# Layer 1 of a four-layer network: TensorE makes the attention scores of batch 0 between the first products of the two batches

## The chip, the cores and the metric

The kernel runs on one NeuronCore of a Trainium2 chip. The metric is the device time of one execution in microseconds (us). The kernel before takes 1194.64 us, the median of three runs (1191.98 to 1196.13).

## The reference

x is (2 batches, 1024 tokens, 256 features), float32. Four layers follow each other, each of the form x = x + ffn(cond(x)). Layer 0 conditions by a low-rank adapter and a layernorm, layers 2 and 3 by a linear map picked by an id of the batch; the ffn parts are mixtures of experts (8 experts in layers 0 to 2, 32 and a shared one in layer 3). The change lies in the conditioning of layer 1, an attention pooling:

```python
attn_in = tanh(einsum('bsd,da->bsa', hidden, W1) + b1)      # a = 64
scores  = einsum('bsa,a->bs', attn_in, v)
mask    = prefix, postfix or all-but-self, by an id of the batch  # (b, 1024, 1024)
p       = softmax(where(mask, scores[:, None, :], -1e30))
pooled  = einsum('bjl,bld->bjd', p, hidden) / count(mask)
```

Layer 1's ffn then routes each pooled token to the one expert with the largest logit (pooled @ Wr + br), with exact gelu, and scales by the gate.

## The kernel before

All of x stays in SBUF as 16 tiles of 128 tokens (x_tok). Work goes by four chunks of 512 tokens: chunks 0 and 1 are batch 0, chunks 2 and 3 batch 1. A product that has to be as exact as float32 is made as three of a cheaper type: each operand is split into a high and a low part, and hi x hi, hi x lo and lo x hi are added (helper mm3, lines 810 to 812; the low parts come from VectorE, line 1653).

Each engine runs its own list of instructions in the order that is written out, and waits on semaphores. There is no planner. For layer 1's conditioning the lists are:

- TensorE: two small products for layer 2's router (L1219, L1222), 32 transposes of x (L822), then for each chunk the attention rows: 6 products, K = 128 features in two halves, 72 output rows (64 of the attention's first matrix and 8 of the router's) by 512 tokens. Chunk c goes to PSUM bank 4 + c. Then for each chunk the scores: 4 matmuls against the vector v give them as columns (L1240, two records each), and one against v broadcast to 128 columns gives the same scores as a row on all 128 partitions (L1242, two records). After chunks 1 and 3 the semaphore s_sc is raised. Then 16 small transposes of the router's rows (L1246) and, batch by batch, the products of the pooling (L1268 to L1280, and mm3).
- ScalarE: the high parts of the transposed x (L1358), then for all four chunks tanh (L1579) and a copy of the 8 router rows (L1580) out of the bank into hidden_f, raising s_chf once for each chunk. Only behind these four pairs stand, for each batch, the copies of the score columns (L1584) and of the score row (L1585), which wait for s_sc. After that the exponentials of the pooling.
- VectorE: the low parts of the transposed x, v broadcast over 128 columns (L2519, raises s_clo), then the splits of x for the pooling (L2530), then the prefix and suffix maxima of batch 0's score row as two scans (L2550, L2551), row maxima, the router's columns (L2539, need the 16 transposes), arguments of the exponentials (L2584), carry_out (L2593, waits for the score rows of both batches), and the same again for batch 1.
- SyncE stores the pooled rows (z_rows) chunk by chunk, and GpSimd gathers them by expert once the slots are known (L701).

The lines that matter for ScalarE's order (1577 to 1585):

```python
for c in range(NC):
    act.wait_ge(s_ch, CH0[1] + c + 1)
    act.activation(HF[0:A0, c, :], PS[0:A0, 4 + c, :], ACT.Tanh, bias=CB1[:, 0:1])
    act.activation(HF[A0:A1R, c, :], PS[A0:A1R, 4 + c, :], ACT.Copy).then_inc(s_chf, 1)
for b in range(B):
    act.wait_ge(s_sc, b + 1)
    bs = slice(b * TPB, (b + 1) * TPB)
    act.activation(SM[:, 0, bs], PS[:, 4 + b, bs], ACT.Copy)
    act.activation(SC[:, 2 * b:2 * b + 2, :], PS[:, 2 * b:2 * b + 2, :], ACT.Copy).then_inc(s_sc_sb, 1)
```

Of the kernel before, what the change touches and what calls it, by code (L numbers as in the profile page):

```python
# [27 lines left out]
NC = B * SEQ // CH  # L28
TPC = CH // P
KD = D // P  # L30
# [37 lines left out]
def build(nc, t):  # L68

    with ExitStack() as ctx:  # L70
# [3 lines left out]
        def sem(name):  # L74
            return ctx.enter_context(nc.semaphore(name))
# [214 lines left out]
        TR0 = {n: KD * NC * i for i, n in enumerate(TR)}  # L290
# [4 lines left out]
        s_tlo = sem("tr_lo")  # L295
# [4 lines left out]
        s_clo = sem("cond_lo")  # L300
        CHI0 = {0: 0, 3: NC}
        CLO0 = {0: 0, 1: NC, 3: NC + 1}
# [504 lines left out]
        def _(pe):  # L807
            def mm3(out, lh, ll, rh, rl, first, last):

                nc.tensor.matmul(out, lh, rh, start=first, stop=False)  # L810
                nc.tensor.matmul(out, lh, rl, start=False, stop=False)  # L811
                return nc.tensor.matmul(out, ll, rh, start=False, stop=last)  # L812
# [410 lines left out]
            last.then_inc(s_red, 1)  # L1223
            transposes("x1", X, lambda c: pe.wait_ge(s_x[c], 16 * 2))
            pe.wait_ge(s_csplit, 2)
            for c in range(NC):
                pe.wait_ge(s_tlo, TR0["x1"] + KD * (c + 1))
                for k in range(KD):
                    w = slice(k * A1R, (k + 1) * A1R)
                    last = mm3(PS[0:A1R, 4 + c, :], W1h[:, 1, w], W1l[:, 1, w], TAh[:, k, c * CH:(c + 1) * CH],  # L1230
                               TAl[:, k, c * CH:(c + 1) * CH], k == 0, k == KD - 1)
                last.then_inc(s_ch, 1)

            pe.wait_ge(s_tlo, TR0["x1"] + KD * NC)
            pe.wait_ge(s_clo, CLO0[1] + 1)
            for c in range(NC):

                pe.wait_ge(s_chf, c + 1)
                for j in range(TPC):
                    nc.tensor.matmul(PS[:, 4 + c // 2, c * TPC + j:c * TPC + j + 1], HF[0:A0, c, j * P:(j + 1) * P],  # L1240
                                     V1[:], start=True, stop=True)
                last = nc.tensor.matmul(PS[:, c, :], SC[0:A0, 7, 0:P], HF[0:A0, c, :], start=True, stop=True)  # L1242
                if c % 2:
                    last.then_inc(s_sc, 1)
            for n in range(NT):
                last = nc.tensor.transpose(PS[:, 6, n * 8:(n + 1) * 8], HF[A0:A1R, n // TPC, n % TPC * P:(n % TPC + 1) * P],  # L1246
                                           ident[A0:A1R, A0:A1R])
# [1481 lines left out]
```

## Time and profile before

| what | value |
|---|---|
| median of 3 runs | 1194.64 us (1191.98 to 1196.13) |
| the profiled execution, time | 1195.43 us |
| its span in the profile | 1193.8 us |
| TensorE matmul busy | 1041.9 us, 87% |
| VectorE busy | 924.3 us, 77% |
| ScalarE busy | 651.1 us, 55% |
| GpSimd busy | 559.4 us, 47% |
| mean granted TensorE clock | 0.921 |

The busy shares say which engine works most over the whole span, the chain of waits which work ended last at each moment, and the timelines what stood idle for what. The granted clock is the share of TensorE's full speed that the chip allowed: 1.00 is 2.4 GHz, 0.50 is 1.2 GHz. Layer 1's attention scores lie near 641 us of the span. In the timelines, a row that ends in brackets gives the idle time before it and what ended that.

### The profile page before, as it was taken

The numbers are of one execution on the slowest core, as the hardware profiler recorded it, in microseconds if no ns is written. First come the engines' busy times: TensorE is split into PE (matmuls) and PEld (weight loads), VectorE is DVE, ScalarE is ACT, GpSimd is POOL, SyncE is SP. The second block draws the span as 40 slices with busy tenths as digits, with TensorE's granted clock in tenths as the row PEclk, the third lists the DMA queues.
The fourth block names the chain that finished last, engine by engine and source line by source line (L and its number), as shares of the span: only waits on it lengthen the run. The fifth ranks groups of instructions, "written<-read, shape, count | busy, mean of one in ns | idle before, by whom it ended". The sixth has DMA issues, their size and how long they took to land.

```text
span 1193.8 us, 26110 instructions
## 1 busy us (share of the span) xinstructions
PE 1041.9 (87%) x7813; PEld 986.1 (83%) x7813; DVE 924.3 (77%) x1570; ACT 651.1 (55%) x1407; POOL 559.4 (47%) x375
## 2 busy tenths in 40 slices
PE   7249999999999999999978749999769958888896
PEld 5238999999999999999966649999669955777785
DVE  7877888888888888888847768875758864967695
ACT  4227776767676767676724447763357625224221
POOL 1312878887888788888740033443046720000000
PEclk9568999999999999999986859999879979999898
DMA  7346787877787777777632167562368743030202
GB/s 216 108 166 207 219 243 215 247 231 234 223 242 234 228 230 235 241 222 234 189 44 71 48 219 266 202 221 84 105 203 261 238 154 122 14 89 24 94 14 71
DMA packets 85093, 206.22 MB, mean 173 GB/s; under 512 B 16738, under 2 KB 58482, under 8 KB 71218
## 3 DMA queue, kind: packets, MB, share of 16 engines
q1 hardware_dynamic: 60530, 161.45, 40.2%
q0 software_dynamic: 24512, 44.19, 15.2%
q8 instruction: 20, 0.33, 0.1%
q14 instruction: 31, 0.25, 0.1%
HBM read 170.85 MB, written 34.75 MB: 172 GB/s over the span
## 4 chain that ended last, share of the span: by engine, by line
PE 73%; DVE 10%; issue 6%; DMA 6%; ACT 2%; POOL 2%; DVEq 0%; POOLq 0%; SPq 0%; ACTq 0%
PE ps L810 22%; PE ps L811 22%; PE ps L812 22%; PE ps L905 2%; DMA z_tok<-in_L_w 1%; DMA w_raw<-z_rows,slot_rows 1%; PE ps L822 1%; DMA y_rows<-w_raw,slot_rows 1%; PE ps L867 1%; DVE hidden_lo L1653 1%; DVE x_tok L1985 1%; POOL w_raw L701 1%; DVE featB_lo L1653 1%; DMA z_tok<-y_rows 1%; DMA x_rows<-w_raw,slot_rows 1%
## 5 line engine op out<-in xcount | busy, mean ns | idle before, releaser
L1419 ACT ACTIVATE hidden_f<-ps,b_block 128x256 f32<-128x256 f32 x480 | 247.6, 516 | 195.0 <-PE ps L812 193.0
L701 POOL DMA_INDIRECT x_tok<-z_gate_rows,slot_rows x88 | 240.4, 2732 | 127.4 <-DVE block_gates L1943 70.2
L1420 ACT ACTIVATE hidden_hi<-ps,b_block 128x256 fp32r<-128x256 f32 x480 | 249.7, 520 | 0.0
L810 PE MATMUL ps<-w_hi,featA_hi 128*128 128x256 f32 (+2 forms) x724 | 209.0, 289 | 8.8 <-DVE scratch L2334 5.5
L811 PE MATMUL ps<-w_lo,featA_hi 128*128 128x256 f32 (+2 forms) x724 | 207.9, 287 | 0.0
L812 PE MATMUL ps<-w_hi,featA_lo 128*128 128x256 f32 (+2 forms) x724 | 207.9, 287 | 0.0
L810 PE MATMUL ps<-featB_hi,hidden_hi 128*128 128x256 f32 x712 | 203.3, 286 | 3.3 <-DVE hidden_lo L1653 3.3
L811 PE MATMUL ps<-featB_lo,hidden_hi 128*128 128x256 f32 x712 | 201.1, 282 | 0.0
L812 PE MATMUL ps<-featB_hi,hidden_lo 128*128 128x256 f32 x712 | 199.7, 280 | 0.0
L1653 DVE TENSOR_TENSOR hidden_lo<-hidden_f,hidden_hi 128x512 fp32r<-128x512 f32 x276 | 178.0, 692 | 17.3 <-ACT hidden_hi L1420 15.6
L729 POOL DMA_INDIRECT x_rows<-w_raw,slot_rows x88 | 145.8, 1657 | 39.9 <-issue 29.0
L810 PEld LDWEIGHTS ps<-w_hi,featA_hi 128*128 128x128 f32 (+2 forms) x724 | 141.1, 195 | 10.6 <-issue 6.3
L811 PEld LDWEIGHTS ps<-w_lo,featA_hi 128*128 128x128 f32 (+2 forms) x724 | 141.3, 195 | 0.4
L812 PEld LDWEIGHTS ps<-w_hi,featA_lo 128*128 128x128 f32 (+2 forms) x724 | 141.3, 195 | 0.3
L810 PEld LDWEIGHTS ps<-featB_hi,hidden_hi 128*128 128x128 f32 x712 | 134.4, 189 | 3.7 <-DVE hidden_lo L1653 3.7
L812 PEld LDWEIGHTS ps<-featB_hi,hidden_lo 128*128 128x128 f32 x712 | 134.6, 189 | 0.0
L811 PEld LDWEIGHTS ps<-featB_lo,hidden_hi 128*128 128x128 f32 x712 | 134.0, 188 | 0.0
L701 POOL DMA_INDIRECT w_raw<-z_rows,slot_rows x44 | 54.3, 1233 | 158.0 <-DVE slot_rows L1818 76.8
L1927 DVE TENSOR_TENSOR w_raw<-ps,b_block 128x256 f32<-128x256 f32 x132 | 54.7, 418 | 69.2 <-PE ps L812 66.7
L1653 DVE TENSOR_TENSOR featA_lo<-scratch,featA_hi 128x2048 fp32r<-128x2048 f32 (+3 forms) x50 | 91.4, 1829 | 3.2 <-ACT featA_hi L1541 2.4
L810 PE MATMUL ps<-w_hi,featB_hi 128*128 128x256 f32 x288 | 84.9, 295 | 8.9 <-DVE w_lo L1653 6.3
L719 POOL DMA_INDIRECT y_rows<-w_raw,slot_rows x44 | 56.5, 1284 | 60.8 <-DVE w_raw L1927 48.4
(487 smaller groups left out, 2591.6 us busy)
## 6 DMA issues: line engine op xcount, KB each, us to landing
scratch<-in_L_w SPq DMA_DIRECT2D x54, 1024.0 KB
z_tok<-in_L_w SPq DMA_DIRECT2D x32, 1024.0 KB
x_tok<-in_L_w SPq DMA_DIRECT2D x22, 1024.0 KB
b_block<-in_L_ffn_b POOLq DMA_DIRECT2D x66, 128.0 KB
z_tok<-y_rows SPq DMA_DIRECT2D x12, 512.0 KB, 5.6
z_tok<-in_L_w SPq DMA_DIRECT2D x12, 512.0 KB
scratch<-in_L_w SPq DMA_DIRECT2D x12, 512.0 KB
z_rows<-z_tok SPq DMA_DIRECT2D x8, 512.0 KB, 2.9
```

What stands on the lines that cost most here:

```text
L701: gp.indirect_dma_start(XBL[L][:, k, tt, :], None, ZD if L else ZD0, bass.IndirectOffsetOnAxis(ap=TOK[:, q * BTT + tt:q * BTT + tt + 1], a ...
L719: gp.indirect_dma_start(YD, bass.IndirectOffsetOnAxis(ap=TOK[:, q * BTT + tt:q * BTT + tt + 1], axis=0), YB[:, k, tt, :], None).then_inc(s ...
L729: gp.indirect_dma_start(XD, bass.IndirectOffsetOnAxis(ap=TOK[:, q * BTT + tt:q * BTT + tt + 1], axis=0), YB[:, k, tt, :], None, compute_op ...
L810: nc.tensor.matmul(out, lh, rh, start=first, stop=False)
L811: nc.tensor.matmul(out, lh, rl, start=False, stop=False)
L812: return nc.tensor.matmul(out, ll, rh, start=False, stop=last)
L822: last = nc.tensor.transpose(PS[:, g % 4, j * P:(j + 1) * P], src[:, c * TPC + j, k * P:(k + 1) * P], ident[:])
L905: last = nc.tensor.transpose(PS[:, 6 + k, m * BT + tt * P:m * BT + (tt + 1) * P], XBL[L][:, k, tt, m * P:(m + 1) * P], ident[:])
L1419: act.activation(HF[:, f // 2, part], ps, func, bias=b1)
L1420: act.activation(HTh[:, k, f // 2, part], ps, func, bias=b1).then_inc(s_hhi[L], 1)
L1653: return nc.vector.tensor_tensor(out, full, hi.bitcast(F32), ALU.subtract)
L1927: nc.vector.tensor_tensor(YB[:, k, j, :], PS[:, 4 + j, 0:D], B2B[:, k, :], ALU.add).then_inc(s_yev[L], 1)
```

## The change

The loops over four chunks on TensorE become two functions. The rows of chunks 0 and 1 are made first, then the two waits for x's low parts and for v, then the scores of chunks 0 and 1, then rows of chunks 2 and 3, then their scores. The instructions are the same, and no other engine's list changes.

```diff
--- before.py
+++ after.py
@@ -1223,7 +1223,7 @@
             last.then_inc(s_red, 1)
             transposes("x1", X, lambda c: pe.wait_ge(s_x[c], 16 * 2))
             pe.wait_ge(s_csplit, 2)
-            for c in range(NC):
+            def attention_rows(c):
                 pe.wait_ge(s_tlo, TR0["x1"] + KD * (c + 1))
                 for k in range(KD):
                     w = slice(k * A1R, (k + 1) * A1R)
@@ -1231,10 +1231,7 @@
                                TAl[:, k, c * CH:(c + 1) * CH], k == 0, k == KD - 1)
                 last.then_inc(s_ch, 1)
 
-            pe.wait_ge(s_tlo, TR0["x1"] + KD * NC)
-            pe.wait_ge(s_clo, CLO0[1] + 1)
-            for c in range(NC):
-
+            def scores(c):
                 pe.wait_ge(s_chf, c + 1)
                 for j in range(TPC):
                     nc.tensor.matmul(PS[:, 4 + c // 2, c * TPC + j:c * TPC + j + 1], HF[0:A0, c, j * P:(j + 1) * P],
@@ -1242,6 +1239,17 @@
                 last = nc.tensor.matmul(PS[:, c, :], SC[0:A0, 7, 0:P], HF[0:A0, c, :], start=True, stop=True)
                 if c % 2:
                     last.then_inc(s_sc, 1)
+
+            attention_rows(0)
+            attention_rows(1)
+            pe.wait_ge(s_tlo, TR0["x1"] + KD * NC)
+            pe.wait_ge(s_clo, CLO0[1] + 1)
+            scores(0)
+            scores(1)
+            attention_rows(2)
+            attention_rows(3)
+            scores(2)
+            scores(3)
             for n in range(NT):
                 last = nc.tensor.transpose(PS[:, 6, n * 8:(n + 1) * 8], HF[A0:A1R, n // TPC, n % TPC * P:(n % TPC + 1) * P],
                                            ident[A0:A1R, A0:A1R])
```

## Rows read from the trace of the kernel before

**Rows 1.** The page, part 4: shares by engine of the chain that ended last.

```profile
PE 73%; DVE 10%; issue 6%; DMA 6%; ACT 2%; POOL 2%; DVEq 0%; POOLq 0%; SPq 0%; ACTq 0%
```

**Rows 2.** Chain of waits, 625 to 700 us: start us, us, what.

```profile
644.22 1.57 PE ps L1242 x2
645.81 0.18 ACT small L1584
645.99 0.92 ACT scratch L1585
646.93 2.29 DVE z_tok L2550
649.23 2.19 DVE z_tok L2551
...
687.79 2.90 DMA z_rows<-z_tok
```

**Rows 3.** Timeline of GpSimd, 680 to 705: start, us, instruction, idle before and releaser.

```profile
700.60 1.03 POOL L701 DMA_INDIRECT w_raw<-z_rows,slot_rows  x1 [76.80 <-DVE slot_rows L1818]
```

**Rows 4.** Timeline of TensorE around the change, 618 to 665.

```profile
630.13 5.75 PE L822 MATMUL ps<-ident,x_tok 128*128 128x128 f32 x32 [2.69 <-DMA x_tok<-x_rows]
635.64 0.47 PE L810 MATMUL ps<-featA_hi,w_hi 128*72 128x512 f32 x1
...
638.29 0.39 PE L812 MATMUL ps<-featA_hi,w_lo 128*72 128x512 f32 x1
...
641.09 0.39 PE L812 MATMUL ps<-featA_hi,w_lo 128*72 128x512 f32 x1
641.41 1.05 PE L1240 MATMUL ps<-cond_v,hidden_f 64*128 64x1 f32 x8
...
643.27 0.95 PE L1240 MATMUL ps<-cond_v,hidden_f 64*128 64x1 f32 x8
644.08 1.69 PE L1242 MATMUL ps<-hidden_f,scratch 64*128 64x512 f32 x2
645.57 1.70 PE L1240 MATMUL ps<-cond_v,hidden_f 64*128 64x1 f32 x8
...
648.98 1.70 PE L1240 MATMUL ps<-cond_v,hidden_f 64*128 64x1 f32 x8
```

**Rows 5.** Timeline of ScalarE, 632 to 665.

```profile
637.92 0.68 ACT L1579 ACTIVATE hidden_f<-ps,cond_b 64x512 f32<-64x512 f32 x1
638.62 0.59 ACT L1580 ACTIVATE hidden_f<-ps 8x512 f32<-8x512 f32 x1
...
642.55 0.59 ACT L1580 ACTIVATE hidden_f<-ps 8x512 f32<-8x512 f32 x1
645.81 0.18 ACT L1584 ACTIVATE small<-ps 128x8 f32<-128x8 f32 x1 [2.67 <-PE ps L1242]
...
652.71 1.02 ACT L1585 ACTIVATE scratch<-ps 128x1024 f32<-128x1024 f32 x1
```

**Rows 6.** Timeline of VectorE, 618 to 665.

```profile
627.56 0.21 DVE L2519 COPY scratch<-cond_v 64x128 f32<-64x128 f32 x1
...
634.48 3.18 DVE L1653 TENSOR_TENSOR featA_lo<-ps,featA_hi 128x512 fp32r<-128x512 f32 x5 [0.17 <-ACT featA_hi L1358]
...
644.20 1.23 DVE L1653 TENSOR_TENSOR w_lo<-x_tok,w_hi 128x1024 fp32r<-128x1024 f32 x1
646.93 2.29 DVE L2550 TENSOR_TENSOR_SCAN z_tok<-scratch 128x1024 f32<-128x1024 f32 x1 [1.51 <-ACT scratch L1585]
...
655.75 0.26 DVE L2539 CAST featB_hi<-ps 128x96 fp32r<-128x96 f32 x1
...
657.79 1.27 DVE L2593 SCALAR_TENSOR_TENSOR hidden_f<-scratch,carry_col,carry_out_mask 16x1024 f32<-16x1024 f32 x1
```

**Rows 7.** Stretches around the change: from:to, us, busy us, PEclk, DMA share, GB/s.

```profile
630.10:634.20 4.10, 4.07 (x19) 4.07 (x20) 1.96 (x3) 2.15 (x4) 0.00 (x0) 0.50 1.00 321
641.10:644.40 3.30, 3.30 (x21) 2.45 (x20) 3.23 (x5) 1.99 (x4) 0.00 (x0) 1.00 0.00 0
644.50:652.60 8.10, 8.10 (x23) 4.81 (x22) 6.45 (x9) 1.09 (x2) 0.00 (x0) 0.50 0.00 0
```

**Rows 8.** Timeline of TensorE in layer 3's conditioning, 975 to 986.

```profile
985.25 0.63 PE L810 MATMUL ps<-featB_hi,w_hi 128*128 128x512 f32 x1
985.68 0.45 PE L811 MATMUL ps<-featB_lo,w_hi 128*128 128x512 f32 x1
```

**Rows 9.** Stretches of dense products at the lower clock in layers 1 and 2.

```profile
723.00:726.30 3.30, 3.30 (x18) 3.30 (x17) 3.27 (x3) 3.18 (x9) 0.00 (x0) 0.50 0.92 367
```

## The prediction

> **What bounds the kernel now.** I read the page's part on the chain that ended last first [rows 1]: TensorE carries 73% of it, so the kernel as a whole is a TensorE kernel. That share says little about the place of the change. So the second view is the chain of waits between layer 0's last scatter and layer 1's first gather [rows 2]. There the reader sees the chain walk from TensorE's score products (L1240, L1242, until 645.8 us) to ScalarE's copy of them out of PSUM (L1584, L1585), then to VectorE's two scans (L2550, L2551) and, 40 us of pooling later, to the store of the last pooled rows (687.79). Nothing in layer 1's experts can begin earlier: GpSimd's first gather waited 76.8 us for the slots that come out of it [rows 3]. A shift of the first scan is thus a shift of the end.
>
> The third view is the timeline of the three engines around the change [rows 4 to 6]. TensorE runs 24 products of the attention rows without a gap (635.64 to 641.09, one each 0.233 us), then the scores of chunks 0, 1, 2, 3. ScalarE, in its own order, loads a table (until 637.92), does tanh and copy of chunks 0 to 3 (pairs 1.31 us apart, the last over at 643.14), and then sits until 645.81. VectorE splits x until 645.43 and idles 1.51 us for the copied score row. So three things end late here, in this order: VectorE's splits 645.43, TensorE's second score 645.77, and the copy.
>
> **The change part by part.** No instruction is added or taken away: 12 row products (chunks 2, 3) move behind the scores of chunks 0 and 1, and two waits move forward with the scores. No DMA is issued by TensorE, so no queue of SP or GpSimd is passed. ScalarE's order is untouched, and that decides the case: its copy of batch 0's scores stands behind tanh and copy of chunks 2 and 3, which now wait for products that TensorE makes last.
>
> Step 1, TensorE reaches the first score. Chunk 1's last row product starts at 638.29 and ends near 638.7 [rows 4]. The score of chunk 0 needs ScalarE's pair for chunk 0, over at 638.62 + 0.59 = 639.21 [rows 5]. TensorE idles about 0.6 us; the table load in front of tanh sets it, not TensorE. The other two waits are free: the last of x's transposed low parts is over at 634.48 + 3.18 = 637.66, and the broadcast vector was made at 627.56 [rows 6]. First score at 639.3 instead of 641.4.
>
> Step 2, the scores of chunks 0 and 1. At full clock one chunk costs 643.27 - 641.41 = 1.86 us, at the lower clock 648.98 - 645.57 = 3.41 us [rows 4]. At full clock they are over at 639.3 + 2 x 1.86 = 643.0, and chunk 1's input (640.52) is there in time. That is 2.8 us earlier than 645.77, and nobody can use it, since ScalarE is not yet at its copy.
>
> Step 3, the rows of chunks 2 and 3: 12 products, 0.233 us each at full clock, 0.43 us at the lower one, from the same shape in layer 3's conditioning [rows 8]. Which level holds is the main unknown. What the rows show: the granted clock stood at 1.00 (2.4 GHz) up to 644.4 and at 0.50 (1.2 GHz) from 644.5 [rows 7], though TensorE never idled half a microsecond in that time. It fell 3.1 us after the last wide product had ended (near 641.3), during scores whose first operand has 64 rows and, in L1240, one column. Back at full level it came at 634.2, 4.1 us after 32 dense transposes had begun [rows 4, 7]. The change puts the same thin scores right behind 12 wide products, with 0.6 us of idleness ahead of them. Two ends:
> - Early fall, the same 3.1 us after the last wide product of chunk 1: 641.6. Then 24% of chunk 1's score at full clock and 76% x 3.41 = 2.6 us at the lower: over at 644.2. The 12 products from 644.2: until a rise 4.1 us later (648.3) there are 9.5 of them, the other 2.5 take 0.6 us: 648.9, and 0.2 us until the last result stands.
> - Late fall, where it was, 644.4: the scores end at 643.0, chunk 2's six products at 644.4, chunk 3's take 6 x 0.43 = 2.6: 647.0, and 0.2.
>
> Step 4, ScalarE. Chunk 2's pair is hidden behind chunk 3's products in both. After the last row product come tanh and copy of chunk 3, 1.3 us, then the score copy. It starts at 649.1 + 1.3 = 650.4 (early fall) or 647.2 + 1.3 = 648.5 (late), instead of 645.8: +4.6 or +2.7 us. VectorE had been waiting for just this copy, so its splits hide none of it. I take the middle, +3.7, since nothing in the rows puts the fall nearer to one end.
>
> Step 5, what follows. Batch 1's scores start near 648.2, behind the row products, and end at 652 at full clock or near 655 at the lower (2 x 3.41 us); their copy is over 1.2 us later, by 656.2. In before it ended at 653.73 [rows 5], and VectorE first needs it at 657.79 [rows 6], in carry_out, a point that moves back by the same 3.7 us to 661.5: 5 us of room, cost 0; if that cover were gone, each microsecond of it would show. The 16 small transposes behind them are needed at 655.75 [rows 6], which moves back too. The pooling is a chain of VectorE and ScalarE, with TensorE's sums of batch 1 released by it; that the clock level meets them at another place I cost at 0, between -1 and +1.
>
> Sum: -0.6 x 0 (TensorE's idleness is off the chain), -2.8 earlier scores x 0, +3.7 later copy = +3.7 us. Profiled execution: 1195.43 + 3.7 = 1199.1. That execution lies 0.79 above the median of 1194.64; against the median 1198.3.
>
> A rule that speaks against this. By the rows, the clock fell at 644.4 with TensorE at work all the time [rows 7]. The Trainium skill (TensorE: Matmul & The Clock Gate, section on why this matters for your kernels) says that long idle gaps between bursts of matmuls are what loses the full clock. By that rule the 0.6 us of waiting would cost nothing and the second batch's rows would run at full clock (the first rival); the trace of before disagrees with it in this very stretch. The same page, section on the back-to-back issue gap, gives some 131 ns for each 512-column matmul; by it the 12 products would take 1.6 us, ScalarE's own two pairs would be the bound (644.0 + 2 x 1.3 = 646.6) and the delay only 0.8 us; the rows show 0.233 us each.
>
> **The rivals.**
> - A, the clock stays full through chunks 2 and 3. For: 12 wide products arrive soon after the scores. Against: it fell in before in a like stretch. The products end at 643.0 + 12 x 0.233 + 0.2 = 646.0, the copy starts at 647.3: +1.5, 1196.1.
> - B, the delay does not reach the end: some later wait has slack. For: layer 1's weights also land after the pooling. Against: their loads are issued behind it, and the gather waited for it [rows 3]. +0, 1194.6.
> - C, faster than before: layer 1's and 2's experts begin at another point of the clock's levels. Dense work of TensorE ran at the lower level at 709.4 to 712.7, 723.0 to 726.3 and 842.5 to 845.8 [rows 9]; each such stretch costs half of 3.3 = 1.65 us. If all three vanish, 3 x 1.65 = 4.95 against +3.7: -1.25, so 1193.4. It decides from the third on. Against: as many new ones can appear.
> - D, batch 1 suffers too: scores and small transposes run at the lower clock and late enough that carry_out waits, 2 us more: +5.7, 1200.3. Against: the room of step 5.
> That the change fails to do what it says is not likely: TensorE has one order, and it is written out.
>
> **How the numbers follow.** Chances: forecast 0.68, A 0.13, B 0.07, C 0.05, D 0.07. What can be told from no change is about 0.3%, 3.6 us. The forecast's own range, 1196.9 to 1199.7, lies on both sides of 1198.2: a little over half of it (0.37) and D count as slower, the other 0.31, A and B as same, which gives 0.44 and 0.51; C and scatter give faster 0.05. The range for 8 in 10 takes in A, most of D and the spread of 4 us among the three times of before: 1194.3 to 1200.9.
>
> **What would show it.** Right: the first L1240 near 639.3; ScalarE's tanh of chunk 2 waiting for TensorE (L812); batch 0's copy (L1585) between 648.5 and 650.5; the first scan equally later; the last store of z_rows later by the same amount; the clock at 0.50 in part of the stretch of chunks 2 and 3. Wrong: the first scan before 646.9 (then ScalarE's order is not what holds it), or a first scan 3 us later with a store of z_rows at its old time (slack that I missed), or the clock at 1.00 until 646 (A).

## The result and the profile after

The changed kernel takes 1199.87 us (median of 8 runs, 1196.76 to 1201.93) against 1194.64 us (8 runs). The ratio to the kernel before is 1.0035, 95% interval 1.002 to 1.005: slower by 4.2 us (2.4 to 6.0); the two medians themselves lie 5.2 us apart. The forecast was +3.7, or 1198.3 us against the median, with a range of 1194.3 to 1200.9.

The two profiled executions differ by only 2.4 us of span, because they were not alike ahead of the change: after began its first transpose of x 1.62 us earlier. So everything below is counted from that transpose (630.13 before [rows 4], 628.51 after). The change has no part in that difference: four variants of the kernel before and of the changed one (e4, e6, e11, e1), whose lists are unchanged up to there, began it at 626.5 to 626.8. The chain of waits of after, start us, us, what:

```profile
641.38 1.92 PE ps L1239 x2
...
648.44 0.59 ACT hidden_f L1588
649.05 0.18 ACT small L1592
649.23 0.92 ACT scratch L1593
650.18 2.29 DVE z_tok L2558
```

Where before the chain went from the score straight to ScalarE's copy [rows 2], tanh and copy of chunk 3 (L1587, L1588) now stand between. (Lines moved: L1237 and L1239 are the old L1240 and L1242, L1587 to L1593 the old L1579 to L1585, L2558 the first scan, the old L2550.) The timeline of TensorE after:

```profile
628.51 5.80 PE L822 MATMUL ps<-ident,x_tok 128*128 128x128 f32 x32 [2.69 <-DMA x_tok<-x_rows]
...
636.71 0.39 PE L812 MATMUL ps<-featA_hi,w_lo 128*72 128x512 f32 x1
637.85 1.02 PE L1237 MATMUL ps<-cond_v,hidden_f 64*128 64x1 f32 x8 [0.75 <-ACT hidden_f L1588]
638.74 1.15 PE L1239 MATMUL ps<-hidden_f,scratch 64*128 64x512 f32 x2
639.68 1.70 PE L1237 MATMUL ps<-cond_v,hidden_f 64*128 64x1 f32 x8
641.25 2.05 PE L1239 MATMUL ps<-hidden_f,scratch 64*128 64x512 f32 x2
643.23 0.70 PE L810 MATMUL ps<-featA_hi,w_hi 128*72 128x512 f32 x1
...
645.86 0.63 PE L810 MATMUL ps<-featA_hi,w_hi 128*72 128x512 f32 x1
...
647.31 0.40 PE L812 MATMUL ps<-featA_hi,w_lo 128*72 128x512 f32 x1
```

The timelines of ScalarE and of VectorE after:

```profile
638.42 0.59 ACT L1588 ACTIVATE hidden_f<-ps 8x512 f32<-8x512 f32 x1
646.10 0.68 ACT L1587 ACTIVATE hidden_f<-ps,cond_b 64x512 f32<-64x512 f32 x1 [7.09 <-PE ps L812]
...
649.05 0.18 ACT L1592 ACTIVATE small<-ps 128x8 f32<-128x8 f32 x1
```

```profile
642.69 1.23 DVE L1661 TENSOR_TENSOR w_lo<-x_tok,w_hi 128x1024 fp32r<-128x1024 f32 x1
650.18 2.29 DVE L2558 TENSOR_TENSOR_SCAN z_tok<-scratch 128x1024 f32<-128x1024 f32 x1 [6.26 <-ACT scratch L1593]
```

And the clock in three stretches after (from:to, us, busy us by engine, PEclk, DMA share, GB/s):

```profile
632.80:639.60 6.80, 6.05 (x36) 4.29 (x35) 6.55 (x13) 5.92 (x10) 0.00 (x0) 1.00 0.01 2
639.70:646.40 6.70, 6.70 (x19) 3.87 (x18) 4.15 (x5) 0.30 (x1) 0.00 (x0) 0.50 0.00 0
646.50:653.20 6.70, 5.99 (x41) 3.96 (x40) 3.02 (x2) 4.32 (x8) 0.00 (x0) 1.00 0.00 0
```

The reader is to see four things. TensorE's scores of batch 0 are over about when the next row product starts, 643.23, and ScalarE doesn't touch them for nearly 6 us: it sits 7.09 us in front of chunk 2's tanh, and its copy comes at 649.05. The level (the granted clock, 1.00 or 0.50) fell near 639.7, as chunk 1's score began, where before it fell within that score's second part, L1242 [rows 4, 7], and 7.5 of the 12 late row products ran at 0.43 us each. VectorE's wait for the score row grew from 1.51 us [rows 6] to 6.26. And the scan stands 21.67 us after the first transpose instead of 16.80: +4.87.

Followed on in the same count: the copy of the last pooled rows starts at 60.94 instead of 56.07, +4.87; GpSimd's first gather at 75.76 instead of 70.47 [rows 3], +5.29. From the gather to the end the profiled execution took 491.9 us against 493.2. So -1.6 ahead of the change, +5.3 to the gather, -1.3 behind it make the +2.4 of the two spans. Only the middle term can be tied to the change. The last one is no larger than what two executions of one kernel differ by: in e5, the changed kernel again, the stretch from the gather to the end took 495.2 us.

### The profile page after: what moved, and what is told of

Same layout as the page of the kernel before. It is cut to its first block, busy times and chain, and to the rows that moved or that the text cites. A ratio compares the mean times of both kernels' runs of the same rounds, so it can differ in the third digit from the quotient of the medians.

```text
span 1196.2 us, 26110 instructions
## 1 busy us (share of the span) xinstructions
PE 1035.9 (87%) x7813; PEld 981.3 (82%) x7813; DVE 924.4 (77%) x1570; ACT 649.7 (54%) x1407; POOL 556.7 (47%) x375
## 4 chain that ended last, share of the span: by engine, by line
PE 70%; DVE 11%; DMA 7%; issue 6%; ACT 3%; POOL 1%; POOLq 1%; DVEq 0%; SPq 0%; ACTq 0%
PE ps L810 22%; PE ps L811 21%; PE ps L812 21%; DMA y_rows<-w_raw,slot_rows 2%; PE ps L905 2%; DMA z_tok<-in_L_w 1%; PE ps L822 1%; DVE featA_lo L1661 1%; PE ps L867 1%; POOL w_raw L701 1%; DVE hidden_lo L1661 1%; DMA z_tok<-y_rows 1%; DMA x_rows<-w_raw,slot_rows 1%; DVE x_tok L1993 1%; DMA w_raw<-z_rows,slot_rows 1%
```

## The experiments

Each was timed in 5 rounds beside the kernel before. The table counts from the first transpose of x in each profiled execution, in us; the ratio is of the times.

Two cautions for the table. The kernel before was profiled once. In e11 nothing differs from it until behind the first scan, and there the scan stands at 17.23 and not at 16.80: the level fell 13.8 us after the first transpose instead of 14.3, ahead of chunk 1's score row (L1242) and not within it. So a difference of 0.4 us between two profiles says nothing by itself. The level must also be alike on both sides of a comparison: in the changed TensorE order it fell 11.2 us after the first transpose in two profiles (changed, e10) and stayed at 1.00 until 20.5 us or later in four (e5, e1, e8, e9), leaving out e3 and e7 with fillers among the scores.

| kernel | first scan | last pooled rows' copy | ratio to before, 95% interval |
|---|---|---|---|
| before | 16.80 | 56.07 | |
| changed | 21.67 | 60.94 | 1.0035 (1.002 to 1.005) |
| e5 changed, again | 18.27 | 57.53 | 1.0039 (1.0016 to 1.0062) |
| e1 ScalarE's order too | 15.10 | 56.07 | 0.9983 (0.9968 to 0.9998) |
| e10 the same, again | 15.94 | 55.61 | 0.9984 (0.9965 to 1.0002) |
| e8 copies behind chunk 2 | 16.82 | 56.13 | 1.0003 (0.9987 to 1.0019) |
| e2 three chunks first | 18.86 | 58.19 | 1.001 (0.9993 to 1.0027) |
| e3 filled | 19.13 | 58.63 | 1.003 (1.0009 to 1.005) |
| e7 both orders, filled | 15.10 | 56.01 | 1.0001 (0.9986 to 1.0017) |
| e6 ScalarE's order alone | 17.24 | 58.39 | 1.0014 (0.9997 to 1.003) |
| e4 copy later | 20.80 | 60.12 | 1.0018 (1.0003 to 1.0034) |
| e9 both orders, pooling filled | 15.06 | 55.37 | 0.9988 (0.9974 to 1.0003) |
| e11 pooling filled alone | 17.23 | 56.49 | 1.0008 (0.9993 to 1.0024) |

**e1, ScalarE's order changed to match.** 

> The changed TensorE order, and ScalarE's list changed to match: tanh and copy of chunks 0 and 1, the copies of batch 0's scores, tanh and copy of chunks 2 and 3, the copies of batch 1's scores. My theory (the loss is ScalarE's copy of batch 0's scores standing behind tanh of chunks 2 and 3, whose products TensorE now makes last): the copy starts when the scores of chunk 1 are over, and the first scan starts when VectorE's splits of x end. Counted from the first transpose of x, the scan was at 16.8 us before and at 21.7 after; here at 15.3 to 15.5. Time 1.4 us under before, 1193.2, some 5.5 under the changed kernel. Rival (TensorE's own order and clock make the loss, whatever ScalarE does): the scan stays near 21 us and the time near 1199.

```diff
-            for c in range(NC): (tanh and copy of chunk c)
-            for b in range(B): (copies of batch b's scores)
+            attention_tanh(0); attention_tanh(1); score_row(0)
+            attention_tanh(2); attention_tanh(3); score_row(1)
```

ScalarE's timeline:

```profile
636.28 0.59 ACT L1588 ACTIVATE hidden_f<-ps 8x512 f32<-8x512 f32 x1
639.48 0.18 ACT L1593 ACTIVATE small<-ps 128x8 f32<-128x8 f32 x1 [2.61 <-PE ps L1239]
```

The first transpose is at 626.59 here: the score copy starts at 12.9 and the scan at 15.10, 0.2 earlier than expected, with VectorE idle no more. The whole of the changed kernel's delay is gone, with TensorE's new order left in. But the level stayed at 1.00 here, and in the changed kernel's first profile it fell, so this pair alone doesn't say how much of the 6.6 us is ScalarE's order. Two pairs with the level alike do: e5 and e1, both at 1.00, have the scan at 18.27 and 15.10 (3.2 us), and the changed kernel and e10, both with the fall at 11.2, at 21.67 and 15.94 (5.7 us; rows at e10). The theory stands and the rival falls. The time is 2 us under before where 1.4 were expected, but the last pooled rows came no earlier than before; e9 looks into that.

**e8, the copies one place later.** 

> The changed TensorE order, ScalarE's copies of batch 0's scores behind tanh and copy of chunk 2 and ahead of those of chunk 3. My theory: the copy waits for six of the late row products and one pair: it starts between 15.6 (full clock) and 18 us (lower clock) after the first transpose, against 15.75 before and 20.6 in the changed kernel; first scan 16.7 to 19, time between -0.1 and +2.3, 1195.8 on average. Rival (position in ScalarE's list is all or nothing): either as the first experiment (15.1) or as the changed kernel (21.7).

```diff
-            score_row(0)
-            attention_tanh(2)
+            attention_tanh(2)
+            score_row(0)
```

The scan at 16.82, between the two, and the time is that of before. The copy starts at 15.7 us, against 15.6 expected for the full level, which this profile has. With the level at 1.00 in all three, the scan stands at 15.10 with the copies behind no late chunk (e1), at 16.82 behind one and at 18.27 behind both (e5): each place in ScalarE's list behind a late chunk costs; it is not all or nothing.

**e2, three chunks first.** 

> TensorE makes the rows of chunks 0, 1 and 2, then the scores of chunks 0 and 1, then the rows of chunk 3, then the other scores. ScalarE's order as in before. My theory: the copy waits for six late products instead of twelve. Rows of three chunks end 4.2 us after the first product, the scores of chunks 0 and 1 at 8.3 to 9.3, the rows of chunk 3 at 9.9 (full clock) to 11.9 (lower clock), then 1.3 us of tanh and copy of chunk 3: the score copy 0.9 to 3.0 us later than before, about half of the changed kernel's delay; time +2, 1196.6. Rival (any split of the row products costs the same, since the wait in front of the first score or the clock's fall is what is paid): +4.

```diff
             attention_rows(1)
+            attention_rows(2)
 ...
-            attention_rows(2)
             attention_rows(3)
```

The scan at 18.86, +2.06 with six late products instead of twelve, all six at the lower level. That is within the expected 0.9 to 3.0. But in e5 (18.27) none and in the changed kernel's first profile (21.67) 7.5 of the late products were slow, so no profile at this one's level tells whether the delay is halved. Time +0.1% (1.2 us), interval from -0.8 to +3.2: it agrees, but the time alone would not tell it from no change.

**e3, fillers to keep the clock up.** 

> The changed kernel with five wide products more (128 x 72 x 512, results never read): three in TensorE's wait ahead of the first score, two between the scores of chunks 0 and 1. If about half of the delay is the lower clock during the rows of chunks 2 and 3, as the prediction has it, and wide products keep the clock up, the twelve row products run at 0.233 us each; the two fillers behind the first score cost 0.5 us themselves: first scan 1.5 + 0.5 = 2 us later than before instead of 4.9, time 1196.6, 3 us under the changed kernel. Rival (the clock has no part in it, or fillers don't hold it): the time is that of the changed kernel or 0.5 us over it.

```diff
             pe.wait_ge(s_clo, CLO0[1] + 1)
+            (3 wide products)
             scores(0)
+            (2 wide products)
             scores(1)
```

The stretch from the rise to the end of all scores, and the scan (first transpose at 627.65):

```profile
631.50:648.40 16.90, 16.90 (x92) 10.52 (x90) 12.66 (x19) 10.29 (x18) 0.00 (x0) 1.00 0.01 1
```

```profile
646.78 2.29 DVE L2562 TENSOR_TENSOR_SCAN z_tok<-scratch 128x1024 f32<-128x1024 f32 x1 [3.94 <-ACT scratch L1597]
```

The level stayed at 1.00 and the scan came at 19.13, +2.3 where 2 were expected. But e5 (next) shows that the changed kernel can keep the level without fillers, so this one profile doesn't prove that the fillers held it, and the time (+0.3%) is not told apart from the changed kernel's. The mechanism's size is shown by e5, the cure is not.

**e5, the changed kernel again.** 

> The changed kernel once more, beside the variants of this call and on their chip. My theory: ratio to the kernel before near 1.0035, +4.2 us; first scan 3.0 to 4.9 us later than before, counted from the first transpose of x (16.8 before), by where the clock falls. Rival (its loss was scatter of the first measurement): ratio at or under 1.001.

No edit. The clock around the change, and the scan (first transpose at 628.24):

```profile
632.10:649.00 16.90, 16.18 (x96) 10.65 (x94) 13.52 (x20) 11.08 (x18) 0.00 (x0) 1.00 0.00 1
649.20:659.20 10.00, 2.65 (x13) 1.76 (x14) 9.51 (x27) 2.19 (x5) 0.00 (x0) 0.50 0.00 0
```

```profile
646.51 2.29 DVE L2558 TENSOR_TENSOR_SCAN z_tok<-scratch 128x1024 f32<-128x1024 f32 x1 [3.08 <-ACT scratch L1593]
```

The same kernel, with the level full through all twelve late products: +1.47 at the scan and +1.46 at the last pooled rows. That is the prediction's rival A to a tenth (+1.5), below what was expected here (3.0 to 4.9), while the ratio repeats, 1.0039. The level is thus a matter of the execution, not of the kernel: 3.4 us lie between the two profiles of one kernel. (Against e11's 17.23 instead of before's 16.80 the delay here would be 1.0 us.)

**e6, ScalarE's order alone.** 

> TensorE's order as in the kernel before, ScalarE's list as in the first experiment: batch 0's score copies ahead of tanh and copy of chunks 2 and 3. My theory (each order must match the other): the copy waits for TensorE's score of chunk 1 as in before, first scan at 16.8 us; chunk 3's tanh is some 6 us later, which delays batch 1's scores to about 27 us, still ahead of their use at 27.7: +0 to +1. Rival (ScalarE's order alone brings what the first experiment gained): -1.4 or more, 0.9988.

The edit of e1 on the kernel before. VectorE's timeline (first transpose at 626.84):

```profile
644.08 2.29 DVE L2558 TENSOR_TENSOR_SCAN z_tok<-scratch 128x1024 f32<-128x1024 f32 x1 [2.06 <-ACT scratch L1586]
...
654.37 0.26 DVE L2547 CAST featB_hi<-ps 128x96 fp32r<-128x96 f32 x1 [1.50 <-PE ps L1246]
```

No gain: the scan at 17.24, and a new wait of 1.50 us for the 16 small transposes behind batch 1's late scores. Those I had thought still in time. The 0.4 at the scan is the lower clock in chunk 1's score, as in e11, and not the edit's. The 2.3 us at the last pooled rows are over the expected 1, the time +0.14% is within reach of it. The rival falls: neither order brings anything alone.

**e4, the copy made later without touching TensorE.** 

> The kernel before, with nothing changed on TensorE; ScalarE copies batch 0's score row four more times, to places nobody reads, ahead of the copy that VectorE waits for: 4 x 0.93 = 3.7 us. My theory (a shift of the first scan is a shift of the end): first scan +3.7, time +3.7, 1198.3. Rival (the delay of the scan is taken up by slack later, and the changed kernel's loss comes from TensorE's clock levels further on): less than +1.5.

```diff
+                if b == 0:
+                    (4 copies of PS[:, 0:2, :] to unused places)
                 act.activation(SC[:, 2 * b:2 * b + 2, :], PS[:, 2 * b:2 * b + 2, :], ACT.Copy).then_inc(s_sc_sb, 1)
```

The scan +4.00, the last pooled rows +4.05: no slack up to there. (Against e11, which has the same fall of the level in chunk 1's score, +3.57 and +3.63; the four copies took 3.6.) The time moved by +0.18%, 2.2 us, interval 0.4 to 4.1, which holds the expected 3.7 but also much less. Up to the pooled rows the passing on is shown; that all of it reaches the end is made likely, not shown, by the times.

**e7, both orders and the fillers.** 

> Both orders changed as in the first experiment, and the five wide products of the third. My theory: the score copy is gated by the scores of chunk 1, half a microsecond later for the two fillers (13.5 instead of 13.0 us), still under VectorE's splits of x, so the first scan stays at 15.1 to 15.3; the clock at full level has nothing left to give on the path: the same time as the first experiment, 0.998 to 0.999. Rival (the clock level kept up helps the pooling behind it): another 1 us or more under it.

The edits of e1 and e3 together. Scan 15.10 as expected, last pooled rows 56.01, time 1.0001 instead of 0.998 to 0.999. The rival, a further gain, falls. A loss of some 2 us against e1 is not told apart from scatter (the intervals overlap).

**e9, the clock kept up in the pooling.** 

> The first experiment's kernel (both orders changed), and in each batch's pooling five products more of 128 x 16 x 240, results never read, behind the first half's twelve wide products, where TensorE idled 0.95 us for the carry. In the first experiment's trace the scan was 1.7 us earlier than before, and the copy of the last pooled rows at the same 56.07 us after the first transpose: the clock fell to 0.50 at 678.0, in the middle of the last 24 products, whose ends VectorE waited 4.41 us for instead of 2.74. Theory (the first experiment's gain is given back there): with the clock kept up the last pooled rows come at 54.4 to 54.6, time 1.6 under the first experiment, 1192 to 1192.5. Rival (the fall there is not prevented or the five products delay the carry): 56 to 56.5, time as the first experiment or a little over.

```diff
+                    if h == 0:
+                        (5 products 128 x 16 x 240 to unused columns)
                     pe.wait_ge(s_plow, plow("carry", b))
```

In e1 the last 24 products straddled a fall:

```profile
671.30:677.90 6.60, 5.64 (x44) 5.00 (x43) 3.88 (x11) 2.85 (x6) 0.00 (x0) 1.00 0.00 0
678.10:682.00 3.90, 3.89 (x17) 3.33 (x15) 0.00 (x0) 1.11 (x4) 0.00 (x0) 0.50 0.39 134
```

and VectorE waited 4.41 us for them, 1.6 longer than in the other profiles, except for e7, the same order with its fillers, where the level fell at the same place and the wait was 4.37:

```profile
677.01 0.16 DVE L2620 TENSOR_TENSOR small<-ps,small 128x4 f32<-128x4 f32 x1 [1.83 <-PE ps L1288]
682.02 0.16 DVE L2620 TENSOR_TENSOR small<-ps,small 128x4 f32<-128x4 f32 x1 [4.41 <-PE ps L1288]
```

With the five products (e9) the level stayed full there, but the rise before it came 3.2 us later in the count, so the first half was the late one:

```profile
678.05 0.16 DVE L2624 TENSOR_TENSOR small<-ps,small 128x4 f32<-128x4 f32 x1 [2.73 <-PE ps L1292]
681.38 0.16 DVE L2624 TENSOR_TENSOR small<-ps,small 128x4 f32<-128x4 f32 x1 [2.74 <-PE ps L1292]
```

The last pooled rows at 55.37: 0.7 of the 1.7 us arrive, not 1.5. Neither theory has it whole. Nor is it shown that the five products kept the level: e10, without them, has it full there as well and a wait of 2.73. The two kernels' times, 0.9988 and 0.9984 (e10), are alike.

**e10 and e11, the controls of e9.** 

> The first experiment's kernel once more, to be compared in one call with the one that fills the pooling, and because one measurement gave 0.9983 and the variant with five wide products in front gave 1.0001. Theory (the scan's 1.7 us are mostly given back in batch 1's pooling): ratio 0.998 to 1.000, last pooled rows at 56 us after the first transpose. Rival (the whole 1.7 us arrive): 0.9986 or less with the last pooled rows at 54.5.

e10 is e1's kernel once more. Its level fell as chunk 1's score began, so the scan came at 15.94 and the last pooled rows at 55.61:

```profile
637.84 1.02 PE L1237 MATMUL ps<-cond_v,hidden_f 64*128 64x1 f32 x8 [0.75 <-ACT hidden_f L1588]
639.68 1.70 PE L1237 MATMUL ps<-cond_v,hidden_f 64*128 64x1 f32 x8
643.22 0.70 PE L810 MATMUL ps<-featA_hi,w_hi 128*72 128x512 f32 x1
```

```profile
643.33 0.18 ACT L1593 ACTIVATE small<-ps 128x8 f32<-128x8 f32 x1 [4.32 <-PE ps L1239]
```

The first transpose is at 628.51, as in the changed kernel's first profile, and TensorE's rows are those of that profile to 0.02 us, through the fall, the rise and the last late product. Only ScalarE's order differs, and its copy starts at 643.33 instead of 649.05. That is the comparison that shows the cause: 5.7 us, with TensorE's order and clock alike. The ratio repeats, 0.9984, which theory and rival both allowed; the last pooled rows lie nearer to the theory's 56, with 0.5 of 0.9 us arriving. What makes the 2 us in the times of e1 and e10 is therefore not shown by their profiles, where the last pooled rows gained 0 and 0.5.

> The kernel before with the five products in each pooling alone. Theory: in the trace of before the clock was full through batch 1's last products, so there is nothing to gain: ratio 1.000, last pooled rows at 56.1 us after the first transpose, within 0.2. Rival (the pooling's clock matters in most executions of before as well): 1.5 us under it.

The fillers on the kernel before bring nothing: 1.0008. The last pooled rows came at 56.49, outside the expected 0.2 about 56.1, because the scan itself was 0.43 later here.

## Why the prediction was right

Steps counted from the first transpose, predicted (early-fall case) and measured in the changed kernel's first profile:

| step | predicted | measured |
|---|---|---|
| TensorE idle ahead of the first score | 0.6 | 0.75 |
| first score | 9.2 | 9.34 |
| clock falls | 11.5 | 11.2 |
| late row products start | 14.1 | 14.72 |
| clock rises again | 18.2 | 18.0 |
| batch 0's copy starts | 20.3 | 20.54 |
| delay of the scan | +4.6 (late fall +2.7, rival A +1.5) | +4.87; in e5 +1.47 |
| delay of the last pooled rows | as the scan | +4.87; in e5 +1.46 |
| time | +3.7 | +4.2 (2.4 to 6.0) |

- **ScalarE's place (steps 2 and 4)** was the cause. e1 and e10 take the loss away by ScalarE's list alone, e10 with TensorE's timeline the same as in the changed kernel's first profile; e8 takes away about half of what e1 does at the same level. TensorE's earlier scores were worth nothing as predicted, since nobody could take them.
- **The level during the late rows (step 3)** was costed as one number between two ends. It is two cases of one kernel, +4.87 and +1.47, and neither profile shows a delay near the middle, +3.7; that this figure came near the measured +4.2 is in part luck. The forecast and rival A were not rivals but two executions of the same program. I gave A 0.13, and of the six profiles whose TensorE list is the changed one up to the late rows four had the level full through the late rows. How often each comes is open: the ratios 1.0035 and 1.0039 would suggest instead that the costly one is the more common. In the two that fell, the level had also risen later, 4.3 us after the first transpose against 3.8 or less; why, the runs don't say.
- **The sizes within step 3** offset each other. The late products began 0.6 us later than costed, and the rise came 3.3 us behind their start instead of 4.1, so 7.5 of them were slow and not 9.5. The 3.1 us from the last wide product to the fall, taken over from before, were 2.7 in the first profile; in e5 the level stood on through chunk 1's score and the late rows.
- **The rule against it.** The Trainium skill (TensorE: Matmul & The Clock Gate, section on why this matters for your kernels) gives long idle gaps between bursts of matmuls as what loses the full clock. The changed kernel's first profile does not agree: the level fell at 639.7 with an idle gap of 0.75 us in front. Nor can its contrary be said outright, since in e5 the same order kept it, with a gap of 0.59. The late row products ran 0.233 us apart in e5, as costed for the full level.
- **The passing on (step 5)**: +4.87 became +4.87 at the last pooled rows and the first gather was 5.29 later; e4 shows the same up to the pooled rows. Batch 1's scores were in time, as costed, but the room is smaller than I made it where they come late: in e6 the 16 transposes behind them were 1.50 us late, which I had named as covered. How much of the delay reaches the end of the kernel is told by the times alone, and only within their intervals.
- **The pooling at another clock phase, costed at 0 between -1 and +1**: right for the changed kernel, too narrow in e1, where 1.7 us gained at the scan were gone at the last pooled rows.
- B (slack later) is against e4's pooled rows. C was not seen: behind the gather the changed kernel took 491.9 and 495.2 us (e5), on both sides of before's 493.2. D was not seen in the changed kernel; in e6 the small transposes were late, as D has it.
- The forecast gave 0.44 to a loss above 0.3% and 0.51 to a smaller one. The measured 0.35%, with its interval of 0.2 to 0.5, lies on that line and bears out neither.

The best version found is e1's: both orders. It was measured at 0.9983 and 0.9984, some 2 us under the kernel before, at the edge of what these runs can tell from no change, and some 6 under the changed one.

## What to carry to other kernels

A result that one engine makes earlier is worth nothing until the engine that takes it has come to that place in its own list; when one engine's order is interleaved, write the consumer's order beside it and look for the item that now waits for the producer's last work. Count from an event just ahead of the change: two executions differed by 1.6 us before the changed lines and by 1.3 us behind them, which would have halved the effect. And where a step depends on TensorE's level, give both levels' results their own chances instead of a middle, because one kernel shows both.

## What the runs showed of the hardware

TensorE's level around thin products (64 rows, one column) is not settled by the kernel: with the same instructions it fell as chunk 1's score began in one execution (0.50 from 639.7 to 646.4) and stayed at 1.00 from 632.1 to 649.0 in another. A second kernel, both orders changed, went the same two ways (e10 and e1). 128 x 72 x 512 products followed each other every 0.233 us at 1.00 and every 0.43 us at 0.50. In the kernel before the level fell near 644.4 with TensorE busy for all of the 3.3 us ahead of it [rows 7].
